# Moving one of two additions of a decoder kernel's ending from VectorE to TensorE

## The chip, the cores and the metric

One Trainium2 chip, one core of it. The metric is the device time of one execution in microseconds (us), as the median of several runs.

## What is computed

One decoder layer on x of shape 16 x 256 x 256 (4096 tokens of 256 features), in fp32:

```python
x = _layernorm(x + linear_attention(x))
x = _layernorm(x + cross_attention(x, ctx))
x = _layernorm(x + ffn(x))          # ffn = attention over batches, then 8 experts of which each token takes 2
```

and inside `ffn`, at its end:

```python
moe_out = einsum("eth,et->th", expert_out, weights)   # two experts of a token, each times its gate
return hidden_after_attn + moe_out
```

so that the very last step is, for each token, `layernorm(resid + y0 + y1)`: `resid` is x plus the attention's result, `y0` and `y1` are the gated results of the token's two experts.

## The kernel before, in words

The kernel is one program of five instruction streams, one per engine, with semaphores set by hand. Its stages follow one another: constants and context keys, two attentions over 16 batches, the second half's attention with the routing in groups of four tiles (a tile is 128 tokens), the experts, and the ending. The experts' stage works through 71 tiles of sorted tokens (`moe_pipeline`, L1633 and on): SyncE loads a tile, TensorE transposes and multiplies, ScalarE and VectorE move data out of the banks, and GpSimd scatters each gated result to its token's row in `results` in HBM, in two halves, y0 and y1 (L1685).

The change is in the ending, L1550 to L1629, which starts when all scatters have landed. It handles the 32 tiles of tokens in ten turns (`TURNS`): 2, 2, six times 4, 2, 2 tiles. In a turn:

- SyncE (`end_sync`) loads y0 and y1 of the turn's tiles into one of four slots (`y_rows`, `DEPTH` = 4; its memory is that of `w1`, so rows call it `all_w`). The loads of turn j wait until turn j-4 is output (`out_ready`).
- VectorE (`end_vector`) adds y1 to y0 (L1613), adds `resid` (L1614), takes the statistics (L155, L158), signals `var_ready`, and then makes the shift of the turn before (`move_mean(j - 1)`, L1605).
- GpSimd (`end_pool`) makes 1/sqrt(var + eps) out of the variance (L1591, L1595).
- ScalarE (`end_scalar`) scales and shifts the rows (L1627), signals `out_ready`, and issues the store of even turns (L1568); SyncE issues that of odd turns, between its loads. A store's access pattern in HBM has 8 as its slowest dimension (`8x16x1024`).

TensorE has nothing to do in the ending before the change. The order in each stream is that of the code; a wait stops what stands behind it on the same engine.

The second half's 8 banks of PSUM (`keep["banks"]`, 128 x 512 fp32 each) serve the experts' stage; in the ending they are free. `const["identity"]` is a 128 x 128 identity in fp32, `const["ident_b"]` one in bf16, `const["hidden_keys"]` a 128 x 512 constant in bf16. `resid` holds `resid` for all tokens in SBUF.

Of the kernel before, what the change touches and what calls it, by code (L numbers as in the profile page):

```python
# [32 lines left out]
ALU = mybir.AluOpType  # L33
# [4 lines left out]
B, N, D = 16, 256, 256  # L38
# [54 lines left out]
def wait(eng, sem, value):  # L93

    if not isinstance(value, int) or value > 0:
        eng.wait_ge(sem, value)
# [779 lines left out]
def part(words, at, *dims):  # L876

    size = int(np.prod(dims))
    names = [f"d{i}" for i in range(len(dims))]
    return words[:, at:at + size].rearrange(f"p ({' '.join(names)}) -> p {' '.join(names)}", **dict(zip(names, dims)))  # L880
# [627 lines left out]
def experts(nc, m, dram, const, keep, weights):  # L1508
# [7 lines left out]
    wide, tables = place("wide", 68, [P, MOE_TILES, E]), place("tables", 70.25, [P, 6, MOE_TILES])  # L1516
# [20 lines left out]
    banks = keep["banks"]  # L1537
# [11 lines left out]
    assert MOE_TILES % 2 == 1  # L1549

    DEPTH, OUTS = 4, 8
    WIDEST = 4
    TURNS = [(0, 2), (2, 2)] + [(first, WIDEST) for first in range(4, TILES - 4, WIDEST)] + [(TILES - 4, 2), (TILES - 2, 2)]
    y_rows = w1[:, :, :].rearrange("p k f -> p (k f)").rearrange("p (i k t d) -> p i k t d", i=DEPTH, k=2, d=D)
    out_rows = w2[:, :, :].rearrange("p (i t) d -> p i t d", i=OUTS)
    en_stats, en_mv = ([part(en_small, first + i * WIDEST * k, WIDEST, k) for i in range(2)]
                       for first, k in ((0, 6), (12 * WIDEST, 2)))
    en_var, en_rstd, en_shift = ([part(en_small, (n + i) * WIDEST, WIDEST) for i in range(2)] for n in (16, 18, 20))
    var_ready, var_done, rstd_ready, shift_ready, out_ready = (
        m.sem(n) for n in ("var_ready", "var_done", "rstd_ready", "shift_ready", "out_ready"))  # L1560
    y_in = [m.sem(f"y_in{i}") for i in range(DEPTH)]
    out_stored = [m.sem(f"out_stored{i}") for i in range(OUTS)]

    def store(eng, j):

        first, wide = TURNS[j]
        eng.wait_ge(out_ready, j + 1)
        eng.dma_start(dram["out_group"][:, :, first:first + wide, :], out_rows[:, j % OUTS, 0:wide, :])\  # L1568
           .then_inc(out_stored[j % OUTS], 16)

    def end_sync(sp):
        for par in range(2):
            sp.wait_ge(ym_out[par], 16 * (LAST // 2 + 1 - par))
        for j, (first, wide) in enumerate(TURNS):
            i = j % DEPTH
            wait(sp, out_ready, j - DEPTH + 1)
            for k in range(2):
                sp.dma_start(y_rows[:, i, k, 0:wide, :], dram["results_of"][k][:, first:first + wide, :])\
                  .then_inc(y_in[i], 16)
            if j >= DEPTH and (j - DEPTH) % 2 == 1:  # L1580
                store(sp, j - DEPTH)
        for j in range(len(TURNS) - DEPTH, len(TURNS)):
            if j % 2 == 1:
                store(sp, j)

    def end_pool(pool):
        for j, (first, wide) in enumerate(TURNS):
# [10 lines left out]
    def end_vector(dve, steps):  # L1598
        V = nc.vector

        def move_mean(j):
            par, wide = j % 2, TURNS[j][1]
            dve.wait_ge(rstd_ready, j + 1)
            wait(dve, out_ready, j - 1)
            V.scalar_tensor_tensor(en_shift[par][:, 0:wide], en_mv[par][:, 0:wide, 0], -1.0, en_rstd[par][:, 0:wide],  # L1605
                                   ALU.mult, ALU.mult).then_inc(shift_ready, 1)

        dve.wait_ge(keep["keep_done"], GROUPS * 2)
        for j, (first, wide) in enumerate(TURNS):
            i, par = j % DEPTH, j % 2  # L1610
            rows, more = y_rows[:, i, 0, 0:wide, :], y_rows[:, i, 1, 0:wide, :]
            dve.wait_ge(y_in[i], (j // DEPTH + 1) * 32)
            steps.chain(V.tensor_tensor(rows, rows, more, ALU.add))  # L1613
            steps.chain(V.tensor_tensor(rows, rows, keep["resid"][:, first:first + wide, 0:D], ALU.add))  # L1614
            wait(dve, shift_ready, j - 1)
            layer_norm_stats(steps, nc, rows, en_stats[par], en_mv[par], var_ready)
            if j > 0:
                move_mean(j - 1)
        move_mean(len(TURNS) - 1)
# [16 lines left out]
    def moe_pipeline(first, step, end, repeat):  # L1636


        first(0, 0, 0)
        step(0, 1, 1)  # L1640
        step(1, 2, 0)
        for j in repeat((MOE_TILES - 5) // 2):
            step(j + 1, j * 2 + 3, 1)
            step(j + 2, j * 2 + 4, 0)
        step(LAST // 2 - 1, LAST - 1, 1, more=False)
        end(LAST // 2, LAST, 0)

    def plain_repeat(eng):
        def repeat(count):
            with eng.Fori(0, count) as j:  # L1650
                yield j
        return repeat
# [188 lines left out]
    def tensor_program(pe):  # L1841
# [68 lines left out]

        pe.wait_ge(s["table_ready"], 1)
        moe_pipeline(first, step, end, plain_repeat(pe))

    return {"sync": sync_program, "gpsimd": gpsimd_program, "scalar": scalar_program, "vector": vector_program, "tensor": tensor_program}

# [158 lines left out]
```

## Time and profile before

| | |
|---|---|
| time, median of 3 runs | 790.93 us (789.56 to 792.3) |
| the profiled execution | 788.46 us, its span 786.5 us |
| busy over the span | TensorE 623.1, VectorE 539.7, ScalarE 389.7, GpSimd 321.6 us |
| the experts' stage ends (last scatter issued) | 729 us |
| the ending | from there to 786.5 us |

Times in rows are us from the span's start, durations in ns where they say mean or min/median/max, else us. "[2.89 <-DMA ...]" behind an instruction is the engine's idle time before it and what ended it. PE is TensorE's matmul, PEld its weight load, DVE VectorE, ACT ScalarE, POOL GpSimd, SP SyncE. An fp32 matmul with two fp32 operands stands as two records; the program's L278 has half as many matmuls as the trace has records of it.

### The profile page before, as it was taken

The page shows a single profiled execution, that of the slowest core. Times are in us where ns is not written, and L with a number is a line of the kernel's source. Part 1 is how long each engine was busy: PE and PEld are TensorE (multiplying, and loading weights), DVE is VectorE, ACT ScalarE, POOL GpSimd, SP SyncE. Part 2 cuts the span into 40 slices and gives each one's busy share as a digit, 9 for nine tenths or more (in the row PEclk, how much of TensorE's full clock was granted, in tenths as well). Part 3 has the DMA queues.
Part 4 walks back from the last instruction along what each step waited for, and adds up shares of the span by engine and source line. Part 5 has one row for each costly group of instructions (what it writes and reads, how often), then busy time and mean ns, then how long its engine had stood idle before and what let it go on. Part 6 is the DMA issues. An engine that isn't in the chain of part 4 may idle for free.

```text
span 786.5 us, 19128 instructions
## 1 busy us (share of the span) xinstructions
PE 623.1 (79%) x5136; PEld 531.3 (68%) x5137; DVE 539.7 (69%) x1852; ACT 389.7 (50%) x923; POOL 321.6 (41%) x439
## 2 busy tenths in 40 slices
PE   5889999999952889888876129999999999999000
PEld 3669989988832667766655118888888888888000
DVE  1357887788844558888875637777777777776583
ACT  1345665656536656655434414555555555554133
POOL 0045767676641012565567721222222222222343
PEclk9999999999975999999876559999999999999555
DMA  6153344434311000111111322222222222221674
GB/s 197 30 161 118 104 122 138 126 97 121 98 25 21 2 2 2 43 56 57 56 56 68 110 82 62 67 81 67 80 68 80 68 79 69 77 71 54 229 265 153
DMA packets 47580, 68.12 MB, mean 87 GB/s; under 512 B 10576, under 2 KB 34256, under 8 KB 47536
## 3 DMA queue, kind: packets, MB, share of 16 engines
q1 hardware_dynamic: 39800, 47.33, 20.7%
q0 software_dynamic: 6480, 17.87, 6.1%
q10 hardware_dynamic: 1256, 2.36, 1.0%
q8 instruction: 24, 0.39, 0.2%
q14 instruction: 20, 0.16, 0.1%
HBM read 40.21 MB, written 23.12 MB: 81 GB/s over the span
## 4 chain that ended last, share of the span: by engine, by line
PE 40%; DVE 14%; issue 4%; ACT 4%; DMA 3%; SPq 2%; another core or an unknown queue 1%; DVEq 0%; ACTq 0%; POOLq 0%
PE half_bank L145 9%; PE half_bank L147 8%; PE half_bank L146 8%; PE half_bank L1865 5%; PE half_bank L1449 4%; PE half_bank L1846 2%; DMA all_w<-results 2%; DVE region_prob L1244 1%; DVE region_h_rows L1266 1%; DVE ba_top L1241 1%; DVE region_en_small L155 1%; PE half_bank L1420 1%; PE half_bank L1434 1%; ACT region_w_hi L896 1%
## 5 line engine op out<-in xcount | busy, mean ns | idle before, releaser
L1685 POOL DMA_INDIRECT results<-all_w_qkv,ex_home x71 | 68.2, 960 | 204.1 <-DVE all_w_qkv L1809 177.3
L1717 ACT ACTIVATE region_hid_hi<-half_bank 128x256 fp32r<-128x256 f32 x142 | 46.8, 381 | 80.4 <-PE half_bank L1865 80.4
L949 POOL DMA_INDIRECT dispatched<-all_xh,all_slot_u x64 | 68.7, 1074 | 37.7 <-DVE all_slot_u L1318 20.5
L145 PE MATMUL half_bank<-region_w_hi,region_hid_hi 128*128 x284 | 80.9, 285 | 2.5 <-DVE region_hid_lo L1801 2.5
L146 PE MATMUL half_bank<-all_w,region_hid_hi 128*128 x284 | 79.6, 280 | 0.0
L147 PE MATMUL half_bank<-region_w_hi,region_hid_lo 128*128 x284 | 79.4, 280 | 0.0
L1704 ACT ACTIVATE all_xh<-half_bank,all_ln_b,all_ln_w 128x128 f32<-128x128 f32 x142 | 57.6, 466 | 23.0 <-PE half_bank L1846 23.0
L1809 DVE TENSOR_SCALAR all_w_qkv<-half_bank,ex_gate 128x256 f32<-128x256 f32 x71 | 34.3, 483 | 48.3 <-PE half_bank L147 47.7
L145 PE MATMUL half_bank<-region_w_hi,region_x_hi 128*128 x142 | 62.5, 440 | 0.5 <-DVE region_x_lo L1794 0.5
L1711 ACT ACTIVATE all_w_proj<-half_bank 128x512 f32<-128x512 f32 x71 | 42.5, 599 | 39.2 <-PE half_bank L147 39.2
L145 PEld LDWEIGHTS half_bank<-region_w_hi,region_hid_hi 128*128 128x128 f32 x284 | 53.2, 187 | 12.9 <-issue 9.5
L147 PE MATMUL half_bank<-region_w_hi,region_x_lo 128*128 x142 | 56.5, 398 | 0.0
L146 PE MATMUL half_bank<-all_w,region_x_hi 128*128 x142 | 56.4, 397 | 0.0
L1801 DVE TENSOR_TENSOR region_hid_lo<-half_bank,region_hid_hi 128x256 fp32r<-128x256 f32 x142 | 53.6, 419 | 1.5 <-ACT region_hid_hi L1717 0.3
L146 PEld LDWEIGHTS half_bank<-all_w,region_hid_hi 128*128 128x128 f32 x284 | 53.4, 188 | 0.5
L147 PEld LDWEIGHTS half_bank<-region_w_hi,region_hid_lo 128*128 128x128 f32 x284 | 53.6, 189 | 0.0
L1846 PE MATMUL half_bank<-all_identity,all_xh 128*128 128x128 f32 x142 | 27.7, 277 | 25.8 <-DMA all_xh<-dispatched 24.7
L1373 PE MATMUL half_bank<-region_xn_t,all_w_qkv 128*64 128x256 f32 x384 | 45.1, 393 | 1.0 <-ACT region_xn_t L1101 1.0
L1865 PE MATMUL half_bank<-all_identity,all_w_proj 128*128 128x128 f32 x284 | 45.1, 281 | 0.7 <-ACT all_w_proj L1711 0.7
L1373 PEld LDWEIGHTS half_bank<-region_xn_t,all_w_qkv 128*64 128x64 f32 x384 | 28.1, 141 | 15.2 <-issue 1.5
L1846 PEld LDWEIGHTS half_bank<-all_identity,all_xh 128*128 128x128 f32 x142 | 17.8, 142 | 26.2 <-issue 24.8
L1865 PEld LDWEIGHTS half_bank<-all_identity,all_w_proj 128*128 128x128 f32 x284 | 30.3, 141 | 7.4 <-issue 4.7
(240 smaller groups left out, 1801.5 us busy)
## 6 DMA issues: line engine op xcount, KB each, us to landing
all_xh<-dispatched SPq DMA_DIRECT2D x71, 130.5 KB
all_w<-in_moe_w_dram SPq DMA_DIRECT2D x32, 256.0 KB, 3.1
all_w<-results SPq DMA_DIRECT2D x12, 512.0 KB, 6.3
all_resid<-at_x SPq DMA_DIRECT2D x32, 128.5 KB
shared_x_t<-in_x_t_dram SPq DMA_DIRECT2D x16, 256.0 KB, 4.2
at_x_tok<-in_x_dram SPq DMA_DIRECT2D x16, 256.0 KB, 4.2
all_w<-results SPq DMA_DIRECT2D x8, 256.0 KB, 3.7
out_dram<-all_w ACTq DMA_DIRECT2D x3, 512.0 KB
```

Of the source, the lines that this page charges most:

```text
L145: nc.tensor.matmul(out, a_hi, b_hi, start=(start and i == 0), stop=False)
L146: nc.tensor.matmul(out, a_hi, b_lo, start=False, stop=False)
L147: ins = nc.tensor.matmul(out, a_lo, b_hi, start=False, stop=(stop and i == len(pairs) - 1))
L949: nc.gpsimd.indirect_dma_start(out=dram["dispatched"], out_offset=bass.IndirectOffsetOnAxis(ap=keep["slot_u"][g % SENDS][:, u, k:k + 1], a ...
L1373: ins = nc.tensor.matmul(out[HALF * i:HALF * (i + 1), :], w_qkv[:, c, which * HALF:(which + 1) * HALF], tiles[:, :, i, :], start=(c == 0), ...
L1685: nc.gpsimd.indirect_dma_start(out=dram["results"], out_offset=bass.IndirectOffsetOnAxis(ap=home[par][:, 0:1], axis=0), in_=ym[par], in_of ...
L1704: ins = nc.scalar.activation(xm_t[par][:, c, :], p_x[:, c, :], ACT.Identity, bias=keep["ln2_b"][:, c:c + 1], scale=keep["ln2_w"][:, c:c + 1])
L1711: nc.scalar.activation(hid[par], p_h[par][:, :], ACT.Gelu_apprx_tanh).then_inc(s["hid_ready"], 1)
L1717: nc.scalar.activation(hid_hi[par][:, cs, :], p_t[half], ACT.Copy).then_inc(s["hid_high"], 1)
L1801: V.tensor_tensor(hid_lo[par][:, cs, :], p_t[half], hid_hi[par][:, cs, :].bitcast(F32), ALU.subtract).then_inc(s["hid_split"], 1)
L1846: ins = nc.tensor.transpose(p_x[:, c, :], xm[par][:, c * P:(c + 1) * P], const["identity"][:, :])
L1865: ins = nc.tensor.transpose(p_t[half][:, c, :], hid[par][:, cols], const["identity"][:, :])
```

## The change

TensorE gets a part in the ending, `end_tensor`, which runs after its last expert tile. It first issues 28 bf16 matmuls into bank 7, whose result nobody reads. Then, for each turn, it waits for the turn's loads, and for each pair of tiles sums y0 and `resid` in a bank: one matmul of the fp32 identity with y0, one with `resid`. Turn j uses one or two of the banks of set j mod 4. A semaphore `sum_mm` says that a turn's banks are full, `sum_read` that VectorE has read them. VectorE now makes one addition for each pair of tiles, bank plus y1, into y0's rows.

```diff
     DEPTH, OUTS = 4, 8
+    KEEP_CLOCK = 28
...
+    SETS = len(keep["banks"]) // 2
...
+    def end_tensor(pe):
+
+        for _ in range(KEEP_CLOCK):
+            nc.tensor.matmul(keep["banks"][7][:, :], const["ident_b"][:, :], const["hidden_keys"][:, :], start=True, stop=True)
+        for j, (first, wide) in enumerate(TURNS):
+            i = j % DEPTH
+            pe.wait_ge(y_in[i], (j // DEPTH + 1) * 32)
+            wait(pe, sum_read, j - SETS + 1)
+            for h in range(wide // 2):
+                bank = keep["banks"][2 * (j % SETS) + h]
+                nc.tensor.matmul(bank[:, :], const["identity"][:, :], y_rows[:, i, 0, 2 * h:2 * h + 2, :], start=True, stop=False)
+                ins = nc.tensor.matmul(bank[:, :], const["identity"][:, :],
+                                       keep["resid"][:, first + 2 * h:first + 2 * h + 2, 0:D], start=False, stop=True)
+            ins.then_inc(sum_mm, 1)
...
-            rows, more = y_rows[:, i, 0, 0:wide, :], y_rows[:, i, 1, 0:wide, :]
+            rows = y_rows[:, i, 0, 0:wide, :]
             dve.wait_ge(y_in[i], (j // DEPTH + 1) * 32)
-            steps.chain(V.tensor_tensor(rows, rows, more, ALU.add))
-            steps.chain(V.tensor_tensor(rows, rows, keep["resid"][:, first:first + wide, 0:D], ALU.add))
+            dve.wait_ge(sum_mm, j + 1)
+            for h in range(wide // 2):
+                tiles = slice(2 * h, 2 * h + 2)
+                sums = keep["banks"][2 * (j % SETS) + h][:, :].rearrange("p (t d) -> p t d", d=D)
+                last = steps.mark(V.tensor_tensor(rows[:, tiles, :], sums, y_rows[:, i, 1, tiles, :], ALU.add))
+            steps.need(last)
+            dve.sem_inc(sum_read, 1)
             wait(dve, shift_ready, j - 1)
...
         moe_pipeline(first, step, end, plain_repeat(pe))
+        end_tensor(pe)
```

On TensorE, behind the last product of the experts' stage, stood nothing; now stand the 28 matmuls and the turns' sums (turns 0 to 3 and the first half of turn 4 are shown; `ex_y_in0` to `ex_y_in3` are the semaphores of the loads):

```order
L1591 MATMUL half_bank7<-all_hidden_keys,all_ident_b 128x512 x28
L1598 MATMUL half_bank0<-all_w1,all_identity 128x512 [waits ex_y_in0]
L1599 MATMUL half_bank0<-all_resid,all_identity 128x512
L1598 MATMUL half_bank2<-all_w1,all_identity 128x512 [waits ex_y_in1]
L1599 MATMUL half_bank2<-all_resid,all_identity 128x512
L1598 MATMUL half_bank4<-all_w1,all_identity 128x512 [waits ex_y_in2]
L1599 MATMUL half_bank4<-all_resid,all_identity 128x512
L1598 MATMUL half_bank5<-all_w1,all_identity 128x512
L1599 MATMUL half_bank5<-all_resid,all_identity 128x512
```

There are 32 such matmuls in all, two for each pair of tiles.

On VectorE, a turn of four tiles in the ending (turn 5), before (-) and now (+):

```order
-L1613 TENSOR_TENSOR all_w1<-all_w1 128x1024 [waits ex_y_in1]
-L1614 TENSOR_TENSOR all_w1<-all_w1,all_resid 128x1024 [waits ex_dve_step]
-L155 BN_STATS region_en_small_2549<-all_w1 128x6 [waits ex_shift_ready,ex_dve_step]
+L1622 SCALAR_TENSOR_TENSOR region_en_small_2549<-region_en_small_2549 128x4 [waits ex_out_ready,ex_rstd_ready]
+L1634 TENSOR_TENSOR all_w1<-half_bank2,all_w1 128x512 [waits ex_sum_mm,ex_y_in1]
+L1634 TENSOR_TENSOR all_w1<-half_bank3,all_w1 128x512
+L155 BN_STATS region_en_small_2549<-all_w1 128x6 [waits ex_dve_step,ex_shift_ready]
 L155 BN_STATS region_en_small_2549<-all_w1 128x6 x3
 L158 BN_AGGR region_en_small_2549<-region_en_small_2549 128x2 [waits ex_dve_step]
 L158 BN_AGGR region_en_small_2549<-region_en_small_2549 128x2 x3
```

The two additions over 1024 elements became two over 512, the first of which also waits for TensorE (`ex_sum_mm`). L1622 is the shift, L1605 before, in the same place. The streams of SyncE, ScalarE and GpSimd are as they were.

## Rows read from the trace of the kernel before

**Rows 1.** The page's first line.

```profile
span 786.5 us, 19128 instructions
```

**Rows 2.** VectorE in time, the ending: start, us, instruction, idle before it.

```profile
734.68 0.69 DVE L1613 TENSOR_TENSOR all_w<-all_w 128x512 f32<-128x512 f32 x1 [6.72 <-DMA all_w<-results]
...
737.95 0.69 DVE L1613 TENSOR_TENSOR all_w<-all_w 128x512 f32<-128x512 f32 x1 [0.72 <-DMA all_w<-results]
...
739.40 0.75 DVE L155 BATCH_NORM_STATS2 region_en_small<-all_w 128x6 f32<-128x256 f32 x2
...
740.56 1.23 DVE L1613 TENSOR_TENSOR all_w<-all_w 128x1024 f32<-128x1024 f32 x1
...
743.07 1.41 DVE L155 BATCH_NORM_STATS2 region_en_small<-all_w 128x6 f32<-128x256 f32 x4
...
744.92 1.22 DVE L1613 TENSOR_TENSOR all_w<-all_w 128x1024 f32<-128x1024 f32 x1
...
749.28 1.22 DVE L1613 TENSOR_TENSOR all_w<-all_w 128x1024 f32<-128x1024 f32 x1
...
760.98 1.23 DVE L1613 TENSOR_TENSOR all_w<-all_w 128x1024 f32<-128x1024 f32 x1 [2.89 <-DMA all_w<-results]
...
765.35 1.22 DVE L1613 TENSOR_TENSOR all_w<-all_w 128x1024 f32<-128x1024 f32 x1
...
770.52 0.69 DVE L1613 TENSOR_TENSOR all_w<-all_w 128x512 f32<-128x512 f32 x1 [0.36 <-DMA all_w<-results]
...
773.04 0.68 DVE L1613 TENSOR_TENSOR all_w<-all_w 128x512 f32<-128x512 f32 x1
```

**Rows 3.** ScalarE in time, the last output.

```profile
777.50 1.09 ACT L1627 ACTIVATE all_w<-all_w,region_en_small 128x256 f32<-128x256 f32 x2 [0.75 <-DVE region_en_small L1605]
```

**Rows 4.** SyncE's loads of turns 4, 5, 9: duration, first and last start; landing.

```profile
L1578 SPq DMA_DIRECT2D all_w<-results x2: 320/376/433, 741.7 to 742.1; - x2
...
DMA to landing us min/median/max: 3.9/5.1/6.4
...
L1578 SPq DMA_DIRECT2D all_w<-results x2: 319/379/439, 746.2 to 746.5; - x2
...
DMA to landing us min/median/max: 4.6/5.4/6.2
...
L1578 SPq DMA_DIRECT2D all_w<-results x2: 319/376/432, 767.6 to 767.9; - x2
...
DMA to landing us min/median/max: 3.0/3.4/3.9
```

**Rows 5.** Windows: us, busy of each engine, PEclk, DMA share, GB/s.

```profile
732.00:742.00 10.00, 0.00 (x0) 0.00 (x0) 6.22 (x15) 1.09 (x2) 2.21 (x4) 0.50 0.91 310
738.00:740.00 2.00, 0.00 (x0) 0.00 (x0) 1.93 (x4) 0.00 (x0) 0.44 (x1) 0.50 0.97 352
772.00:778.00 6.00, 0.00 (x0) 0.00 (x0) 3.51 (x13) 3.93 (x8) 2.75 (x5) 0.50 0.50 160
```

**Rows 6.** TensorE in time; L1266 on VectorE; fp32r products of 512 columns.

```profile
28.16 1.20 PE L278 MATMUL ck_p_set<-ck_k_t,ck_b_q_cols 128*128 128x308 f32 x4
29.20 1.20 PE L278 MATMUL ck_p_set<-ck_k_t,ck_w_q 128*128 128x308 f32 x4
...
L1266 DVE TENSOR_TENSOR region_h_rows<-half_bank,all_resid 128x512 f32<-128x512 f32 x16 | 11.1, 691 | 23.5 <-PE half_bank L1449 16.2 <-POOL all_resid L1052 4.5 <-DVE region_h_rows L1266 2.7
...
700.71 0.39 PE L145 MATMUL half_bank<-region_w_hi,region_x_hi 128*128 x1
700.93 0.40 PE L146 MATMUL half_bank<-all_w,region_x_hi 128*128 x1
```

**Rows 7.** Windows for the clock: about 730, and about 252.

```profile
727.00:729.00 2.00, 0.44 (x4) 0.23 (x2) 0.48 (x1) 0.00 (x0) 0.27 (x1) 1.00 0.18 66
...
730.00:731.00 1.00, 0.00 (x0) 0.00 (x0) 0.00 (x0) 0.00 (x0) 0.00 (x0) 0.58 0.37 131
...
252.00:256.00 4.00, 4.00 (x22) 2.47 (x23) 0.34 (x1) 1.29 (x4) 0.00 (x0) 0.54 0.00 0
```

More of the change, by code:

```diff
@@ L1558, in experts @@
     en_var, en_rstd, en_shift = ([part(en_small, (n + i) * WIDEST, WIDEST) for i in range(2)] for n in (16, 18, 20))
-    var_ready, var_done, rstd_ready, shift_ready, out_ready = (
-        m.sem(n) for n in ("var_ready", "var_done", "rstd_ready", "shift_ready", "out_ready"))
+    var_ready, var_done, rstd_ready, shift_ready, out_ready, sum_mm, sum_read = (
+        m.sem(n) for n in ("var_ready", "var_done", "rstd_ready", "shift_ready", "out_ready", "sum_mm", "sum_read"))
+    SETS = len(keep["banks"]) // 2
     y_in = [m.sem(f"y_in{i}") for i in range(DEPTH)]
```

## The prediction, made before the changed kernel ran

> **What bounds the kernel now.** The execution shown has a span of 786.5 us [rows 1]. The change touches only its end, so I read, in this order, VectorE's and ScalarE's instructions in time, the queue's loads, the windows for the DMA share, and last TensorE's clock.
>
> VectorE [rows 2]: a four-tile (wide) turn has two additions, 740.56 to 743.07 (2.51 us), then statistics and the shift, 743.07 to 744.92 (1.85), together 4.36 us; turns follow one another without a wait up to 758. A two-tile (narrow) turn has 1.45 us of additions (737.95 to 739.40) and 1.16 us of the rest. VectorE then waits for results at 760.98 (2.89 us) and 770.52. So the first half looks bound by VectorE; the second half by the loads. It is a loop: turn j is loaded when turn j-4 is output, and the shift of a turn stands on VectorE behind the statistics of the next turn. The last output starts at 777.50 [rows 3], 9 us before the span's end.
>
> Loads [rows 4]: turns 0 to 3 are loaded up front; VectorE starts turns 2 and 3 without a wait, so I take them as landed when TensorE comes to them. From the last issue to the last landing, turn 4: 742.1 + 6.4 = 748.5. Turn 5: 746.5 + 6.2 = 752.7. Turn 9, with little ahead of it: 767.9 + 3.9 = 771.8.
>
> DMA [rows 5]: while only loads run, the share is 0.91 at 310 GB/s, at best 0.97 at 352. From 772 on only stores are under way, and the share is 0.50 at 160 GB/s: a store keeps half of the engines busy, and the others stand still. The Trainium skill, page "DMA: Bandwidth & Descriptors", section on queues, rings and completion order, says that a copy uses the largest engine count up to 16 that divides its slowest dimension; the store's is 8, and by that rule the trace's half share is no accident but a ceiling for every store. In the ending 4.19 MB are stored: at 160 GB/s 26.2 us. 8.39 MB are loaded: at 352 GB/s 23.8 us. Together 50.0 us for the engines that do both, and the ending from 732 to 786.5 has 54.5. **Whatever VectorE saves, no more than some 4 us can be had**, and the lull between the first loads and the first stores takes part of that.
>
> **The change part by part.**
>
> *VectorE.* It loses one of two additions. A 128x512 addition with one operand in a bank takes 0.691 us [rows 6], as long as one from SBUF. A wide turn's additions become 2 x 0.69 + 0.03 = 1.41 us in place of 2.51, a narrow turn's 0.72 in place of 1.45. The turn is now 1.41 + 1.85 = 3.26 us, or 0.72 + 1.16 = 1.88. Over six wide and four narrow turns 9.5 us of work go.
>
> *TensorE.* 32 matmuls of 128x512 in full fp32 are new. The nearest row is the fp32 matmul of 128x308 [rows 6]: each stands as two records, and four records take 29.20 - 28.16 = 1.04 us, so 0.52 us a matmul, and 0.52 x 512/308 = 0.86 us for 512 columns. The fp32r product [rows 6], one record with 0.39 us and some 0.23 from start to start, is the other end; the program has plain fp32 on both operands, so I take 0.86. Two matmuls fill a bank (1.71 us, a narrow turn), four a wide turn (3.42 us). That is more than the 1.10 us that VectorE saves in the turn, and **VectorE waits for all of it**: the bank isn't read before both operands went through.
>
> *The wait.* Behind VectorE's wait for the bank stand its own statistics and the shift of the turn before, so ScalarE's output, the store, and the load of four turns later wait too. The wait of TensorE for a bank set to be read is free: four sets, and VectorE has read the set long before.
>
> *The 28 matmuls.* bf16, 128x512, at about 0.22 us: 6.2 us from 727.4 to 733.6, on an engine that stood idle, before the first landing at 734.68. Cost nothing; if that cover were gone, each would cost its 0.22.
>
> *The walk at full clock.* S is TensorE's end, E the end of VectorE's turn; each load is first left at its old time from issue to landing. Turn 0: S 736.4. Turn 1: S 737.95 + 1.71 = 739.7, E 741.6, against 740.56: 1.0 late, and so is output 0 and load 4. Turn 2: S 744.0, E 747.3 against 744.92: output 1 and load 5 are 2.3 late. Turn 3: S 747.4, E 750.7 against 749.3: load 6 is 1.4 late. Turn 4: landed 749.5, S 752.9, E 756.2 (2.5 late). Turn 5: landed 755.0, S 758.4, E 761.7, against 758.0: load 8 is 3.6 late. Turn 6: landed 762.4, S 765.8, E 769.1 against 765.35: load 9 is 3.7 late. Turn 7: S 769.2. Turn 8: landed 774.1, S 775.8, E 777.7. Turn 9: S 777.5, additions done 778.4 against 774.5 (773.04 and 1.45): **3.9 us late at the end**. That is the upper end at full clock. From below: time to landing is mostly queueing (3.9 us for turn 9, 6.4 for turn 4), and loads that are issued later meet less ahead of them; at best they land as before and the walk costs nothing. Between 0 and 3.9 I take 2.5, nearer to the walk, since the stores keep half of the engines busy anyway.
>
> *The clock.* The windows [rows 7] show the granted clock full after the last matmul (727.4) until 730.2, then at 1.2 GHz: about 2.7 us idle were enough. At 252 TensorE was at the low level and worked without a break for 3.7 us before it had 2.4 GHz again (0.54 over 252 to 256). In the walk TensorE idles 747.4 to 749.5 and 752.9 to 755.0 (2.1 us each, too short by these rows) and 758.4 to 762.4 and 769.2 to 774.1 (4.0 and 4.9, long enough). Turn 6 then takes 3.7 + (3.42 - 1.85) = 5.3 us, 1.9 more. Turns 8 and 9 take 3.4 us each and not 1.7: S of turn 9 becomes 780.9, 3.2 later than 777.7, and this reaches the end whole. One fall before turns 8 and 9: 3.2; none: 0; I take 3.0. [...]
>
> **Sum:** 2.5 + 3.0 = 5.5 us. The profiled execution's own time is 788.46 (span and 2.0 us around it), so 794.0 in its terms; the median of the runs shown is 790.93, 2.5 above it, and I give **796.4 us**.
>
> **The rivals.**
> - *The clock stays full.* The matmuls bridge every gap, and only the walk counts: +2.5, 793.4 us. For it: two of four gaps are short. Against: the other two are longer than the one at 727.4.
> - *The clock stays low almost throughout.* Then a wide turn costs 6.8 us on TensorE, which becomes the bound: S 738.1, 741.5, six wide turns to 782.5, 789.3; VectorE's last additions would begin 16 us after 773.04, less what the idle queues give back: +15, 806 us. Against: unbroken work brought the clock back at 255.7.
> - *It cancels.* Loads take up all of the lateness, the short falls hit turns that wait anyway: +0.5, 791.4 us.
> - *Faster.* VectorE is the bound up to 758, and TensorE's sums run ahead under its statistics. This decides if a matmul takes under (4.36 - 3.26)/4 = 0.28 us, which fp32r has (0.23) and fp32 (0.86) has not; or if TensorE, once it is ahead, hides behind the turns. Outputs then come earlier and fill the DMA lull; of the 4 us at most 2.5 come out: 788.4 us.
>
> **How the numbers follow.** A measurement of this kernel tells about 0.3%, 2.4 us, from no change. Forecast 0.56, clock full 0.15, low throughout 0.07, cancels 0.14, faster 0.08. Slower by over 2.4: the forecast (less 0.01), the low clock, and somewhat over half of the full-clock case, 0.70. Faster: 0.07. Within: 0.23. The range goes from the cancelling case, 791.4, to the forecast with the skill's rule and a full 3.9 from the walk (790.93 + 3.9 + 3.2 + 2.0 = 800.0) and 1.5 for the spread of runs: 801.5.
>
> **What would show it.** VectorE's additions at 0.69 us, but waiting for TensorE at nearly every turn; TensorE's wide turn at 3.4 us or more; the granted clock at 1.2 GHz in turns 6 and 8; loads of turns 4 to 9 issued 1 to 4 us later; the last output starting 780 to 784 and not 777.50; the share at 0.5 after it. It is wrong if VectorE still goes from turn to turn without a wait up to turn 5, if a pair of matmuls takes well under 1.7 us, or if the last load is issued at 767.6 or earlier.

## The result, and the profile after

The changed kernel took 800.44 us (median of 4 runs, 793.71 to 805.16), the kernel before, in the same comparison, 791.62 us (4 runs, 789.56 to 792.74): a ratio of 1.0105, 95% interval 1.006 to 1.015. A second comparison, the first experiment below, has more runs: 1.0068, 1.0037 to 1.0098. The change makes the kernel slower, by 5 to 8 us.

The profiled execution has a span of 796.8 us, against 786.5 [rows 1]. Where do the 10.3 us lie? The last scatter of the experts' part marks the start of the ending in both kernels. GpSimd in time, the changed kernel, that scatter:

```profile
735.62 0.96 POOL L1707 DMA_INDIRECT results<-all_w_qkv,ex_home  x1 [2.22 <-DVE all_w_qkv L1831]
```

In the kernel before, that scatter was issued at 728.73. So **6.9 us of the 10.3 arose before the ending**, where the two programs are the same, and 3.4 in it: from the scatter to the span's end it is 57.8 us before and 61.2 after. Most of them, 5.9 us, arose in the first 60 us: a load of the next batch that the kernel before issues at 63.43 us is issued 5.9 us later. Windows of the changed kernel and, in the second fence, of the kernel before, with PEclk, the DMA share and GB/s as the last three columns:

```profile
34.00:36.00 2.00, 0.12 (x1) 0.00 (x0) 0.48 (x1) 0.63 (x1) 0.19 (x3) 1.00 0.00 0
36.00:38.00 2.00, 0.64 (x3) 0.67 (x4) 0.00 (x0) 0.00 (x0) 1.22 (x1) 0.54 0.00 0
38.00:40.00 2.00, 2.00 (x11) 2.00 (x11) 0.00 (x0) 0.00 (x0) 0.00 (x0) 0.50 0.63 196
42.00:44.00 2.00, 2.00 (x8) 1.51 (x7) 0.91 (x1) 1.14 (x4) 0.36 (x1) 0.75 0.29 110
```

```profile
34.00:36.00 2.00, 0.28 (x2) 0.31 (x3) 0.00 (x0) 0.16 (x1) 1.26 (x1) 1.00 0.00 0
36.00:38.00 2.00, 2.00 (x16) 1.88 (x15) 0.00 (x0) 0.64 (x2) 0.00 (x0) 1.00 0.46 139
38.00:40.00 2.00, 2.00 (x10) 1.35 (x8) 0.69 (x1) 1.71 (x5) 0.63 (x1) 1.00 0.82 219
42.00:44.00 2.00, 1.49 (x13) 1.49 (x14) 0.75 (x3) 0.00 (x0) 0.00 (x0) 1.00 0.32 83
```

TensorE idled in both around 34 us; this time it lost its clock there, and took the first batch's products at 1.2 GHz. In the endings that follow I therefore count from the last scatter. "Ending" below is that length.

VectorE in the ending, the additions of turn 0 (two tiles), of turns 2 and 3 (four tiles, with the statistics of turn 2), of turn 6 and of the last turn (answers to [rows 2]):

```profile
743.60 0.69 DVE L1634 TENSOR_TENSOR all_w<-half_bank,all_w 128x512 f32<-128x512 f32 x1 [8.75 <-PE half_bank L1599]
...
751.27 1.29 DVE L1634 TENSOR_TENSOR all_w<-half_bank,all_w 128x512 f32<-128x512 f32 x2 [2.33 <-PE half_bank L1599]
752.71 1.41 DVE L155 BATCH_NORM_STATS2 region_en_small<-all_w 128x6 f32<-128x256 f32 x4 [0.15 <-DVE all_w L1634]
...
754.71 1.29 DVE L1634 TENSOR_TENSOR all_w<-half_bank,all_w 128x512 f32<-128x512 f32 x2
...
775.37 1.29 DVE L1634 TENSOR_TENSOR all_w<-half_bank,all_w 128x512 f32<-128x512 f32 x2 [7.48 <-PE half_bank L1599]
...
786.26 0.69 DVE L1634 TENSOR_TENSOR all_w<-half_bank,all_w 128x512 f32<-128x512 f32 x1 [1.65 <-PE half_bank L1599]
```

An addition of 512 columns takes 0.69 us, as from SBUF, and two take 1.29 (one of 1024 from SBUF took 1.22); a turn of four repeats after 3.44 us (751.27 to 754.71) and not 4.36. But VectorE waits for TensorE ahead of it: 2.33 us at turn 2, 7.48 at turn 6. The waits over the whole ending, engine, line, for whom, us in total, times, longest:

```profile
POOL region_en_small L1608 <- DVE region_en_small L1622: 29.2, 8, 9.5
DVE all_w L1634 <- PE half_bank L1599: 25.1, 8, 8.8
PEld half_bank L1598 <- DMA all_w<-results: 20.6, 8, 6.2
PE half_bank L1598 <- DMA all_w<-results: 14.3, 7, 5.3
```

The wait of VectorE for loads [rows 2] is gone from this list; 25.1 us of waits for TensorE stand in its place, and TensorE in turn waits for the loads. TensorE itself, the 28 matmuls, turn 2, and turns 6 and 8 (to be read beside [rows 6]: two records for one matmul):

```profile
734.16 6.22 PE L1591 MATMUL half_bank<-all_hidden_keys,all_ident_b 128*128 128x512 bf16 x28
...
747.46 1.13 PE L1598 MATMUL half_bank<-all_w,all_identity 128*128 128x512 f32 x2 [0.61 <-DMA all_w<-results]
748.43 1.02 PE L1599 MATMUL half_bank<-all_resid,all_identity 128*128 128x512 f32 x2
749.28 1.02 PE L1598 MATMUL half_bank<-all_w,all_identity 128*128 128x512 f32 x2
750.14 1.02 PE L1599 MATMUL half_bank<-all_resid,all_identity 128*128 128x512 f32 x2
...
769.73 2.08 PE L1598 MATMUL half_bank<-all_w,all_identity 128*128 128x512 f32 x2 [5.34 <-DMA all_w<-results]
771.60 1.91 PE L1599 MATMUL half_bank<-all_resid,all_identity 128*128 128x512 f32 x2
773.31 1.09 PE L1598 MATMUL half_bank<-all_w,all_identity 128*128 128x512 f32 x2
...
780.52 1.13 PE L1598 MATMUL half_bank<-all_w,all_identity 128*128 128x512 f32 x2 [1.83 <-DMA all_w<-results]
```

Turn 2 takes 0.86 us a matmul, 747.46 to 751.00 for four and the start of the next; VectorE starts at 751.27, **3.8 us after the first of them**. At turn 0 it is 2.1 us (741.48 to 743.60). Before turn 6 the engine sat idle for 5.34 us, and its first two matmuls take 1.9 and 1.7 us: the granted clock was 0.50 from 768 to 772 (windows of the same kernel, beside [rows 7]):

```profile
766.00:768.00 2.00, 0.00 (x0) 0.00 (x0) 1.77 (x9) 0.32 (x2) 0.00 (x1) 0.66 0.69 219
768.00:770.00 2.00, 0.27 (x1) 0.27 (x2) 0.00 (x0) 1.99 (x4) 1.26 (x2) 0.50 1.00 381
770.00:772.00 2.00, 2.00 (x3) 0.91 (x4) 0.00 (x0) 0.00 (x0) 0.00 (x0) 0.50 0.80 290
772.00:774.00 2.00, 2.00 (x4) 0.79 (x3) 0.00 (x0) 0.00 (x0) 0.00 (x0) 0.64 0.67 210
774.00:776.00 2.00, 2.00 (x6) 0.81 (x5) 0.64 (x2) 0.00 (x0) 0.00 (x0) 1.00 0.53 192
```

It came back after 3.6 us of unbroken work, and this cost turn 6 1.8 us: 5.6 from its first matmul to VectorE's addition (769.73 to 775.37), where turn 2 has 3.8. It stayed full at turns 8 and 9, where the gaps were 1.8 and 1.7 us. ScalarE's last output (beside [rows 3]), and the load of turn 9 (beside [rows 4]):

```profile
790.13 1.09 ACT L1649 ACTIVATE all_w<-all_w,region_en_small 128x256 f32<-128x256 f32 x2 [0.75 <-DVE region_en_small L1622]
```

```profile
L1580 SPq DMA_DIRECT2D all_w<-results x2: 319/376/432, 780.9 to 781.2; - x2
...
DMA to landing us min/median/max: 2.6/2.7/2.9
```

From the scatter, the last output starts at 54.5 us, against 48.8 before: 5.7 us late. The end is only 3.4 late: the tail behind the last output's start shrank from 9.0 to 6.7 us. That fewer stores still stood in line is the likely reason; no run shows it.

### The profile page after: what moved, and what is told of

Same layout as the page of the kernel before. It is cut to its first block, busy times and chain, and to the rows that moved or that the text cites. A ratio compares the mean times of both kernels' runs of the same rounds, so it can differ in the third digit from the quotient of the medians.

```text
span 796.8 us, 19325 instructions
## 1 busy us (share of the span) xinstructions
PE 667.7 (84%) x5228; PEld 552.5 (69%) x5229; DVE 531.2 (67%) x1848; ACT 390.6 (49%) x923; POOL 311.2 (39%) x439
## 4 chain that ended last, share of the span: by engine, by line
PE 34%; issue 27%; DMA 3%; SPq 2%; DVE 2%; ACT 1%; ACTq 0%; DVEq 0%; POOLq 0%
PE half_bank L145 9%; PE half_bank L147 9%; PE half_bank L146 8%; PE half_bank L1887 5%; DMA all_w<-results 2%; PE half_bank L1868 2%; PE half_bank L1598 1%; ACT all_w L1649 1%; PE half_bank L1599 1%; SPq L1680 1%; DVE region_en_small L155 1%; DVE all_w L1634 1%; SPq L1681 0%; SPq L1580 0%; DMA results<-all_w_qkv,ex_home 0%
## 5 line engine op out<-in xcount | busy, mean ns | idle before, releaser
L1726 ACT ACTIVATE all_xh<-half_bank,all_ln_b,all_ln_w 128x128 f32<-128x128 f32 x142 | 57.8, 467 | 23.0 <-PE half_bank L1868 22.9
L1831 DVE TENSOR_SCALAR all_w_qkv<-half_bank,ex_gate 128x256 f32<-128x256 f32 x71 | 34.3, 483 | 49.5 <-PE half_bank L147 48.8
L146 PE MATMUL half_bank<-all_w,region_x_hi 128*128 x142 | 56.8, 400 | 0.0
L1649 ACT ACTIVATE all_w<-all_w,region_en_small 128x256 f32<-128x256 f32 x32 | 16.8, 589 | 42.3 <-DVE region_en_small L1622 42.3
```

Of the source, the lines that this page charges most:

```text
L146: nc.tensor.matmul(out, a_hi, b_lo, start=False, stop=False)
L1726: ins = nc.scalar.activation(xm_t[par][:, c, :], p_x[:, c, :], ACT.Identity, bias=keep["ln2_b"][:, c:c + 1], scale=keep["ln2_w"][:, c:c + 1])
```

## The experiments

Each kernel is compared with the kernel before on the same chip; the chips differ by up to 14 us in the kernel before itself, so only ratios are compared, and lengths of endings within profiles. A ratio of 1.001 is 0.8 us. An ending is that of one profiled execution: the two of the changed kernel are 2.3 us apart.

| run | ratio to before, 95% interval | ending, us | last output from scatter, us |
|---|---|---|---|
| before | 1 | 57.8 | 48.8 |
| the changed kernel, first profile | 1.0105 (1.006 to 1.015) | 61.2 | 54.5 |
| e1, the changed kernel again | 1.0068 (1.0037 to 1.0098) | 63.5 | 56.8 |
| e2, resid first | 1.0021 (0.9992 to 1.005) | 59.0 | 49.9 |
| e3, without the 28 matmuls | 1.0087 (1.0059 to 1.0115) | 61.6 | 53.2 |
| e4, before with one addition | 0.996 (0.9933 to 0.9987) | 54.8 | 45.5 |
| e5, matmuls in the waits | 1.0043 (1.0008 to 1.0077) | 61.1 | 52.6 |
| e6, one matmul a bank | 1.0038 (1.0009 to 1.0068) | 60.1 | 52.9 |
| e8, changed, wide stores | 0.9988 (0.9951 to 1.0025) | 58.8 | 51.9 |
| e9, before, wide stores | 0.9952 (0.9926 to 0.9977) | 52.7 | 45.7 |
| e10, before, even stores by GpSimd | 1.0044 (1.0022 to 1.0067) | 59.0 | 50.5 |
| e11, resid first, even stores by GpSimd | 1.0055 (1.0025 to 1.0086) | 61.0 | 51.4 |
| e12, resid first, bank by bank | 1.0013 (0.9992 to 1.0034) | 57.1 | 48.9 |
| e13, e12 with wide stores | 0.9929 (0.9902 to 0.9955) | 55.4 | 48.6 |

### e1: is the first part's 6.9 us the change's?

No edit. Expected:

> The changed kernel once more, unaltered. In its profile the last scatter was issued at 735.6 us and not at 728.7, so 6.9 us of the 10.3 us between the two spans lay ahead of the ending, where the program is the same; TensorE ran at 1.2 GHz from 36 to 43 us there and did not before. Theory A (the part ahead of the ending is the clock's chance, the change itself costs what the ending shows, 3.4 us in that profile and up to 6 where the clock falls more often): over five rounds 3 to 7 us slower than before, the scatter's time free to vary, the ending 60.5 to 64 us long against 57.8. Theory B (the change slows the whole program): the last scatter again some 7 us late, the difference 8 to 10 us.

5.3 us slower by the ratio (2.9 to 7.7), in the middle of theory A's range; theory B's 8 to 10 us lie above it. The last scatter was issued at 727.20, 1.5 us earlier than in the kernel before, but that says little, since the chips differ. On the chip of e1 the programs without TensorE's part have it at 721.7 (e4), 721.1 (e9) and 720.7 (e10), and those with it at 721.0 (e2), 719.5 (e11), 726.0 (e3) and 727.2 (e1). So TensorE's part does not by itself make it late. In the two late ones the clock was lost at 38 us again (0.50 over 38 to 40 in e1, over 40 to 42 in e3); in e4, which has nothing of the change, it was lost for a shorter time (0.50 over 38 to 40, 0.72 over 40 to 42). Theory B falls as far as these go. What decides whether the clock is lost there stays open. The ending was 63.5 us, and shows what the first profile did not:

```profile
758.00:761.00 3.00, 0.00 (x0) 0.00 (x0) 1.66 (x9) 1.19 (x3) 1.03 (x2) 0.90 0.92 311
761.00:764.00 3.00, 2.91 (x4) 1.37 (x5) 0.00 (x0) 0.88 (x2) 0.24 (x1) 0.50 0.80 285
764.00:767.00 3.00, 3.00 (x5) 1.16 (x4) 0.00 (x0) 0.00 (x0) 0.00 (x0) 0.50 0.62 226
767.00:770.00 3.00, 3.00 (x8) 1.33 (x7) 1.93 (x4) 0.00 (x0) 0.00 (x0) 0.97 0.45 178
779.00:782.00 3.00, 1.02 (x2) 0.00 (x0) 1.61 (x6) 0.60 (x2) 0.00 (x0) 0.50 0.51 178
```

Here the clock was low for some 7 us before and in turn 6, where 6.8 us went by from the first matmul to VectorE's addition, and again at turn 9, after TensorE had sat idle for 3.57 us; turn 8 ran at full clock. So two executions of the same kernel lose it at different turns. The spread of the runs doesn't come from this alone: it is 11 us for the changed kernel and 3 for the kernel before in the first comparison, of 4 runs each, but 9.1 for both in the second, of 12 and 35.

### e2: resid ahead of the landing

```diff
+        residual(0)
+        residual(1)
         for j, (first, wide) in enumerate(TURNS):
             i = j % DEPTH
             pe.wait_ge(y_in[i], (j // DEPTH + 1) * 32)
-            wait(pe, sum_read, j - SETS + 1)
             for h in range(wide // 2):
-                nc.tensor.matmul(bank[:, :], const["identity"][:, :], y_rows[:, i, 0, 2 * h:2 * h + 2, :], start=True, stop=False)
-                ins = nc.tensor.matmul(bank[:, :], const["identity"][:, :],
-                                       keep["resid"][:, first + 2 * h:first + 2 * h + 2, 0:D], start=False, stop=True)
+                ins = nc.tensor.matmul(keep["banks"][2 * (j % SETS) + h][:, :], const["identity"][:, :],
+                                       y_rows[:, i, 0, 2 * h:2 * h + 2, :], start=False, stop=True)
             ins.then_inc(sum_mm, 1)
+            if j + 2 < len(TURNS):
+                residual(j + 2)
```

`residual(j)` waits for `sum_read` and issues the matmuls of `resid`. Expected:

> TensorE puts resid into a turn's banks before it waits for the turn's loads, two turns ahead, and only y0 follows the landing. The same 32 matmuls, but half of them off the way from landing to VectorE, and work in the waits. Theory A (the price is TensorE's 3.4 us between landing and VectorE): a wide turn waits 1.7 us and not 3.4; the ending 57.5 to 59 us, 3 us less than the changed kernel's 61.2, about as long as before. Rival C (TensorE's amount of work or bank traffic is the price, wherever it lies): no gain over the changed kernel.

59.0 us, and 1.6 us slower than before (the interval includes none) where the changed kernel, in the same comparison, is 5.3: theory A. TensorE's work is the same; what counts is how much of it stands between a landing and VectorE. A better clock isn't the reason: e2 ran turns 8 and 9 at 1.2 GHz, and its last output still starts nearly 3 us earlier than that of e5 below, which kept 2.4 GHz throughout. Rival C falls.

### e3: without the 28 matmuls

```diff
-    KEEP_CLOCK = 28
+    KEEP_CLOCK = 0
```

> The 28 matmuls ahead of the first turn are left out; nothing else. Theory A: the clock is at 1.2 GHz when the first loads land, turns 0 and 1 take 3.4 us each and the wide turn after them 5 us, the ending is 1 to 3 us longer than the changed kernel's, 62 to 64. Rival D (the waits put the clock down anyway, the 28 matmuls buy nothing): the same length within 1 us.

61.6 us, between the two profiles of the changed kernel, and 1.0087 against 1.0068: 1.5 us, inside both intervals. Theory A's 62 to 64 us were missed, and rival D isn't excluded: whether the 28 matmuls are worth anything stays open. TensorE did start turn 0 at the low level (0.58 from 728 to 731, then 0.50), which put VectorE's first addition 1.7 us later from the scatter than in the first profile, but it had the clock back at turn 1, and turn 2 began 0.4 us earlier than there.

### e4: what VectorE's saving is worth alone

```diff
             steps.chain(V.tensor_tensor(rows, rows, more, ALU.add))
-            steps.chain(V.tensor_tensor(rows, rows, keep["resid"][:, first:first + wide, 0:D], ALU.add))
```

The result lacks the residual. Expected:

> The kernel before with the addition of resid in the ending left out (so the residual is missing from the result): VectorE has 1.25 us less in a wide turn, TensorE nothing to do. This is the most that the change could bring. Theory E (the eight engines that carry loads and stores bound the ending): 1.5 to 3.5 us faster than before, the ending 54.5 to 56.5 us, VectorE waiting for loads at most turns. Rival F (VectorE bounds the ending up to turn 5 and the gain comes out whole): 6 us or more faster.

3.1 us faster, the ending 54.8: **10.4 us less work on VectorE are worth 3** (six wide additions of 1.25 and four narrow ones of 0.73). It waits for loads now; its waits at turns 4, 6 and 8:

```profile
740.45 1.23 DVE L1613 TENSOR_TENSOR all_w<-all_w 128x1024 f32<-128x1024 f32 x1 [1.10 <-DMA all_w<-results]
...
750.21 1.22 DVE L1613 TENSOR_TENSOR all_w<-all_w 128x1024 f32<-128x1024 f32 x1 [3.46 <-DMA all_w<-results]
...
761.41 0.69 DVE L1613 TENSOR_TENSOR all_w<-all_w 128x512 f32<-128x512 f32 x1 [4.91 <-DMA all_w<-results]
```

Theory E; rival F falls.

### e5: the clock held through the ending

```diff
+    FILL = [4, 4, 0, 8, 0, 18, 0, 6, 5, 0]
...
-    SETS = len(keep["banks"]) // 2
+    SETS = 3
...
             ins.then_inc(sum_mm, 1)
+            for _ in range(FILL[j]):
+                nc.tensor.matmul(keep["banks"][7][:, :], const["ident_b"][:, :], const["hidden_keys"][:, :], start=True, stop=True)
```

> The changed kernel with bf16 matmuls in TensorE's waits of the ending too: 4, 4, 8, 18, 6 and 5 of 0.22 us behind the sums of turns 0, 1, 3, 5, 7 and 8, into bank 7, and three sets of banks in place of four so that bank 7 is free for them. Theory A (two prices: the sums between landing and VectorE, and the clock that the waits lose): the granted clock stays at 2.4 GHz through the ending, turn 6 takes 3.4 us and not 5 to 7, the ending is 1.5 to 3 us shorter than the 61.2 and 63.5 us of the two profiles of the changed kernel, some 60; still longer than 57.8. Rival G (the clock costs nothing at the end, since the loads or stores cover it): the same length as the changed kernel.

```profile
767.00:770.00 3.00, 2.58 (x10) 1.07 (x8) 0.84 (x7) 2.01 (x4) 1.26 (x2) 1.00 0.94 332
770.00:773.00 3.00, 2.47 (x6) 0.76 (x4) 0.42 (x1) 0.06 (x1) 0.00 (x0) 1.00 0.67 228
779.00:785.00 6.00, 4.78 (x13) 1.93 (x13) 3.26 (x15) 3.12 (x7) 2.15 (x4) 1.00 0.63 189
```

VectorE's addition of turn 9:

```profile
784.72 0.69 DVE L1637 TENSOR_TENSOR all_w<-half_bank,all_w 128x512 f32<-128x512 f32 x1 [0.80 <-PE half_bank L1600]
```

The clock stayed at 2.4 GHz through all turns. The last output started 52.6 us after the scatter: 3.9 later than in the kernel before, where the prediction's walk at full clock has 3.9. The changed kernel's two profiles have 54.5 and 56.8, so by these profiles the clock costs 1.9 and 4.2 us there. Part of the 3.9 is the fill's own: the five matmuls behind turn 8 held TensorE until 782.73, and the loads of turn 9, issued at 778.5 at the latest and landed within 3.8 us, were there by 782.3. That is 0.4 us at least. The end of e5 is at 61.1 and not at 60: its stores stood in line for 8.5 us behind the last output's start, where the first profile had 6.7. The ratio, 1.0043, is 3.4 us, against 5.3 of e1: the difference of 1.9 us goes the expected way, and is within both intervals. The ending of e5 is also no shorter than that of the first profile, so rival G isn't excluded: the profiles show that the clock moves the last output, and not that it moves the end.

### e6: half of the work

The matmul of `resid` left out, so the residual is missing from the result:

```diff
-                nc.tensor.matmul(bank[:, :], const["identity"][:, :], y_rows[:, i, 0, 2 * h:2 * h + 2, :], start=True, stop=False)
-                ins = nc.tensor.matmul(bank[:, :], const["identity"][:, :],
-                                       keep["resid"][:, first + 2 * h:first + 2 * h + 2, 0:D], start=False, stop=True)
+                ins = nc.tensor.matmul(bank[:, :], const["identity"][:, :], y_rows[:, i, 0, 2 * h:2 * h + 2, :],
+                                       start=True, stop=True)
```

> Only y0 goes through the identity, resid is left out: one matmul for each bank in place of two, so 13.7 us of TensorE's 27.3 at full clock, the same waits (the residual is missing from the result). Theory A: like resid first, 1.7 us between landing and VectorE in a wide turn, the ending 57.5 to 59.5 us, 0 to 3 us slower than the kernel before, although VectorE has the whole saving. If it is the passage through a bank as such (semaphores, bank reads) that costs, it stays at 61 or more.

60.1 us: a miss by 0.6 in the length, and more in the reason. I had halved the work and forgotten the clock:

```profile
744.00:748.00 4.00, 2.25 (x3) 0.68 (x4) 1.61 (x5) 0.00 (x0) 0.96 (x2) 0.53 1.01 383
760.00:764.00 4.00, 3.19 (x5) 1.17 (x4) 3.12 (x11) 0.52 (x2) 0.15 (x1) 0.50 0.82 266
772.00:776.00 4.00, 2.82 (x4) 1.09 (x4) 2.94 (x10) 0.00 (x0) 0.00 (x0) 0.50 0.68 246
```

With half of the matmuls TensorE idled more: it ran at 1.2 GHz in turn 1, in part of turns 2 and 4, all through turns 5 to 7, and in turn 9. Half of the work at half of the rate is what the whole was at full rate. The last output still started 1.6 us earlier than in the first profile of the changed kernel, and the ratio is 3.0 us against 5.3, within both intervals: halving the work gained less than expected, not nothing. The ending of e4, which has as much work on VectorE and none on TensorE, is 5.3 us shorter.

### e7, e8, e9: stores over all engines

```diff
-        dram["out_group"] = dram["out"].rearrange("(t b i) d -> b t i d", t=B, b=P // B)
+        dram["out_group"] = dram["out"].rearrange("(p i) d -> p i d", p=P)
```

and the store's index accordingly; the rows stand in another order of the tokens. e9 is the kernel before with it (in the place of e7, which had the same aim and has no run), e8 the changed kernel. Expected of e9 and e8:

> The kernel before, each store written to rows in another order of the tokens, so that its slowest dimension is 128 and not 8 (same 4 KB runs and bytes; the result's rows stand in the wrong places). Theory E (eight engines carry the stores and bound the ending): the stores spread over all 16, the tail behind the last output's start shrinks from 9 to under 6 us, the ending 52 to 54.5 us against 57.8, 3.5 to 5.5 us faster. Rival F (VectorE and the landing times bound it): under 2 us, and only in the tail. The changed kernel with the same stores had 58.8 us: the difference between the two is the change's price without this ceiling, 3 to 6 us by theory A.

> The changed kernel with the same stores as the experiment before (rows in the wrong places). Theory E: with the DMA no longer in the way, the change's price is TensorE's way alone: the ending 56 to 60 us, 3 to 5 us shorter than the changed kernel's, and still 3 to 6 us longer than the kernel before with these stores.

The tail of e9, and that of the kernel before, which has 0.48 at 154 GB/s over 772 to 784:

```profile
763.00:770.00 7.00, 0.00 (x0) 0.00 (x0) 2.20 (x8) 3.99 (x8) 2.46 (x4) 0.50 0.55 225
```

```profile
772.00:784.00 12.00, 0.00 (x0) 0.00 (x0) 3.51 (x13) 4.52 (x9) 2.75 (x5) 0.50 0.48 154
```

e9: the ending 52.7 us, 5.1 less, 3.8 us by the ratio; the last output starts 3.1 us earlier (turn 6's additions start 29.4 us after the scatter and not 32.3), so the narrow stores had also held up the loads, and the tail is 7.0 us in place of 9.0 (under 6 was expected). Theory E, with one thing beside it: the issue of a store of four tiles also takes 0.36 us on its engine in place of 0.62, and the rows lie elsewhere in HBM; no run has one without the others. With these stores the changed kernel's profile has 58.8, in which TensorE ran at 1.2 GHz in part of turn 7. The two profiles are 6.1 us apart (theory A's upper edge was 6), where with narrow stores it was 3.4 and 5.7; the ratios, 0.9988 and 0.9952, are 2.8 us apart, less than the 5.3 with narrow stores. Whether the stores' ceiling hid part of TensorE's price stays open.

### e10, e11: stores by GpSimd

```diff
-            if j % 2 == 0:
-                store(act, j)
...
+            if j >= 2 and j % 2 == 0:
+                store(pool, j - 2)
+        store(pool, len(TURNS) - 2)
```

> The kernel before, the stores of even turns issued by GpSimd, two turns later in its stream, in place of ScalarE; the result complete. If GpSimd's queue puts a store's eight shares on other engines than those of SyncE's, the load evens out: 1 to 4 us faster, the share behind the last load over 0.55. If it takes the same eight, or if the issue holds GpSimd up (its pow feeds the shift): the same or up to 5 us slower.

> TensorE's sums with resid first, and the stores of even turns by GpSimd. If the stores' engines are the ceiling that resid-first meets (59.0 us with VectorE waiting less than in the changed kernel), 1 to 4 us shorter than that, 55 to 58 us; if GpSimd is held up by the issue, 59 or more.

Both slower: 59.0 and 61.0 us, the second branch of each expectation. The first store is issued 6.2 us later than in the kernel before (19.2 us after the scatter and not 13.0), the next two 5.1 later, the last one 2.5. Behind the landing of the last load, at 767.2, e10 has:

```profile
767.00:770.00 3.00, 0.00 (x0) 0.00 (x0) 2.43 (x7) 0.16 (x1) 0.07 (x1) 0.50 0.90 190
```

So the share rose over the 0.50 of the kernel before, as for stores that run on other engines than SyncE's, but 0.90 moved only 190 GB/s, where 0.50 moved 160 in the kernel before [rows 5] and 0.55 moved 225 in e9. Up to turn 7 VectorE was 3.3 us ahead of the kernel before; then it waited 3.07 and 2.71 us for the loads of turns 8 and 9. Late issue and slower stores both fit, and these runs don't part them.

### e12, e13: bank by bank

e2's order, and `sum_mm` counts banks, each addition of VectorE waiting for its own:

```diff
+                nc.tensor.matmul(keep["banks"][2 * (j % SETS) + h][:, :], const["identity"][:, :],
+                                 y_rows[:, i, 0, 2 * h:2 * h + 2, :], start=False, stop=True).then_inc(sum_mm, 1)
...
-            dve.wait_ge(sum_mm, j + 1)
             for h in range(wide // 2):
+                dve.wait_ge(sum_mm, first // 2 + h + 1)
```

> Resid first, and VectorE may read each bank as soon as its own sum is there, not when the whole turn's is. A wide turn's way from landing to VectorE's first addition is one matmul, 0.86 us, in place of 3.4 in the changed kernel and 1.7 with resid first. Theory A: the ending 56.5 to 58.5 us, at or just under the 57.8 of the kernel before, since the saving of VectorE (54.8 with one addition and nothing in its place) now stands against 0.9 us a turn. Rival C (the way to VectorE is not what costs): 59 or more, as with resid first.

> The same with the stores spread over all 16 engines (rows in the wrong places). Theory A and E together: 50.5 to 53.5 us, against 52.7 of the kernel before with these stores and 58.8 of the changed kernel with them. If VectorE's work is worth anything once the stores are out of the way, this one is the first that shows it: under 52.7.

e12: 57.1 us and 1.0013: no difference from the kernel before. In turn 4 the time from TensorE's first matmul behind the landing to VectorE's addition went from 3.8 (changed) to 2.1 (e2) to 1.2 us, and the price from 5.3 to 1.6 to 1.0 us: theory A, though the last two can't be told apart, or from nothing. e13 is 5.6 us faster than before by the ratio (6 runs), e9 3.8; but its profile has 55.4, a miss of the 50.5 to 53.5 expected, against e9's 52.7, with the clock at 0.57 for one turn. The two intervals overlap, so it stays open whether TensorE's sums help once the stores are wide. No version with all rows in their places beat the kernel before.

## Why the prediction was right

The forecast was 796.4 us, 5.5 over the median, in a range of 791.4 to 801.5. Measured were 800.44 in the first comparison, 1.05% or 8.3 us, and 0.68% in the second, 5.3 us (2.9 to 7.7). The mechanism is the one forecast: VectorE waits for TensorE behind each landing, and TensorE loses its clock in the waits. How well the single terms fit is less sure than the sum.

- **VectorE's saving.** 0.69 us an addition, as taken. The turn takes 3.44 us in place of the 3.26 forecast: 0.15 us between the additions and the statistics was not in the sum. So VectorE saves 8.0 us (six turns of 0.92, four of 0.61) and not 9.5. At most "some 4 us can be had": e4 has 3.1, and e9 bears out the reason given, stores on half of the engines. The Trainium skill's rule for the number of engines stands on the page that the prediction names, "DMA: Bandwidth & Descriptors", but in the section "Why a DMA increments its semaphore by 16 and not by 1", and it wants a number that divides the slowest dimension of both sides of the copy.
- **TensorE's matmuls.** 0.86 us as taken from L278, 3.54 us for four (0.1 more at a turn's start). But VectorE starts 3.8 us after the first of them, and not 3.4; in a narrow turn 2.1, not 1.7. The sum had 0.4 us too little in each turn here.
- **The wait.** VectorE waited for TensorE at eight turns, and loads 4 to 9 were issued later. On the first profile, moved by the scatter's 6.9 us: turn 6 landed 1.9 us late (forecast 1.4), turn 8 3.1 (3.6). The last load was issued 6.4 us late, beyond the 1 to 4 among the signs.
- **The walk at full clock.** Its upper end of 3.9 us is what e5's last output has, in part by luck: the walk lacks 0.4 us a turn, and e5 has at least 0.4 us of its own fill in it. I took 2.5 of the 3.9 for the time, since later loads would land sooner; e5 has 3.3 in the ending and 3.4 by the ratio. That is 0.9 us over the 2.5, but with the fill's share taken off and an interval of 0.6 to 6.1 us the runs don't show that the term was too small. The reason for taking less was not borne out at turn 6: its load was issued at 760.6 and took 9.1 us, as before. One step was right without its premise: the walk takes turn 2 as landed when TensorE comes to it (739.7), yet starts it at 740.56. The trace has it waiting 0.61 us for that landing, at 11.8 us after the scatter, just where VectorE started turn 2 before.
- **The clock.** It fell before turn 6, as forecast, and cost that turn 1.8 us (forecast 1.9). Of the fall before turns 8 and 9, e1 has half, at turn 9, and the first profile nothing. For 3.0 us taken, e1 less e5 gives 1.9 by the ratios, and the last outputs 1.9 and 4.2: the size isn't settled. The range's upper end holds 2.0 us for a low clock at turns 4 and 5. No run of the changed kernel shows that term: TensorE idled 2.35 us before turn 4 and ran it and turn 5 at 2.4 GHz. The Trainium skill, page "TensorE: Matmul & The Clock Gate", section on HAM oscillation, describes a kernel whose DMA waits are long enough to throttle TensorE, so that every burst of matmuls between them starts throttled. Turn 6, behind 5.34 us of idle time, agrees; the section doesn't say it of shorter waits, and behind 2.35, 1.83 and 1.66 us (turns 4, 8 and 9) the first profile has full clock.
- **The 28 matmuls.** 6.2 us as taken, and hidden. They ended at 740.4 and turn 0 began at 741.48 at full clock.

So 5.5 against 5.3 is closer than the terms deserve: 0.4 us a turn was missing, the two sizes were picked inside wide bounds, and the runs don't settle either. The first comparison lies 3 us above the second. Its profile shows the clock lost in the first 60 us, which no step of mine treated, beyond 1.5 us for the spread of runs. Whether the four runs of that comparison lost it there too stays open; only one has a profile.

The rivals: "faster" hung on a matmul under 0.28 us or on TensorE hiding behind the turns; neither was so. "The clock stays full", +2.5, is e5, and has 3.4 (0.6 to 6.1). "Low almost throughout" and "cancels" were not seen.

## What to carry to other kernels

Work that moves to an idle engine is free only where it doesn't stand between an arrival and its reader: here 3.8 us between landing and VectorE cost more than 8 us of saved VectorE time gained, of which e4 shows that only some 3 could come out. Do first what doesn't hang on the arrival, and hand over piece by piece; that took the price from 5 us to 1. And before an engine's share of a stage is cut, look at the DMA share behind the last load: it was 0.5 here, the stores ran on half of the engines, and spreading them was worth about as much (3.8 us) as half of VectorE's additions (3.1).

## What was not expected of the hardware

GpSimd's two small operations of a turn took a fifth and half of the time while VectorE's additions read a bank. In the kernel before, `L1591` and `L1595` of a turn of four take 1.11 and 1.98 us while VectorE adds two operands from SBUF; in the changed kernel, beside VectorE's additions from a bank (754.71 to 756.00, above):

```profile
754.76 0.23 POOL L1608 TENSOR_SCALAR region_en_small<-region_en_small 128x4 f32<-128x4 f32 x1 [4.69 <-DVE region_en_small L1622]
755.08 1.04 POOL L1612 TENSOR_TENSOR region_en_small<-region_en_small,all_minus_half 128x4 f32<-128x4 f32 x1
```

```profile
745.12 1.11 POOL L1591 TENSOR_SCALAR region_en_small<-region_en_small 128x4 f32<-128x4 f32 x1 [1.51 <-DVE region_en_small L1605]
746.32 1.98 POOL L1595 TENSOR_TENSOR region_en_small<-region_en_small,all_minus_half 128x4 f32<-128x4 f32 x1
...
758.20 0.23 POOL L1591 TENSOR_SCALAR region_en_small<-region_en_small 128x4 f32<-128x4 f32 x1 [1.19 <-DVE region_en_small L1605]
758.51 1.04 POOL L1595 TENSOR_TENSOR region_en_small<-region_en_small,all_minus_half 128x4 f32<-128x4 f32 x1
```

The last two lines are of the kernel before with VectorE idle: 0.23 and 1.04, the same as in the changed kernel with VectorE busy. No wait for GpSimd was on the way to the end in either kernel except the last turn's 1.2 us, so this gained nothing here. The Trainium skill, page "SBUF — State Buffer", section "SBUF: two separate sides", says that VectorE with two operands from SBUF and GpSimd share a pair of ports, of which one of them holds the whole until its instruction ends; the rows agree in that the second operand's place decides, and I hadn't counted it.

The second is e6: with half of TensorE's matmuls gone the ending is 60.1 us, little under the 61.2 with all of them, because the clock went with the work.
